# Local attention: VectorE copies the odd tiles' output out of PSUM at the head of a later iteration, ScalarE the even ones

## The chip, the cores and the metric

The kernel runs on one core of one Trainium2 chip. The time is the device's, in microseconds (us), from launch to end. The engines are named as the profile names them: PE (matrix multiply; PEld its weight loads), DVE (vector), ACT (scalar), POOL (GpSimd), SP (which here only issues DMAs). Each engine runs its own instructions in order and waits on semaphores.

## What is computed

Two recurrent blocks of a model over x of shape (4, 1024, 128), float32. Each block is `x = x + s * silu(f)`, where s is an attention branch and f a second branch, both of the layer-normed x. The change lies in the second branch of the second block: two layers (DEPTH = 2) of local attention with 8 heads of 64 channels and a window of 64, each followed by a gated feed-forward. Cut to what matters:

```python
h = shift_token(x)                      # second half of the channels comes from the token before
q, k, v = split(h @ wqkv)               # 8 heads x 64
q, k = rotary(l2norm(q) * qs, l2norm(k) * ks)
sim = einsum('bhwid,bhwjd->bhwij', bq, bk)      # 64 queries x 128 keys
attn = softmax(where(mask, -max, sim))
o = einsum('bhwij,bhwjd->bhwid', attn, bv)
x = x + o @ wo
h = layernorm(shift_token(x)) * lg + lb
...
x = x + (a * gelu(g)) @ w2 + b2
```

## The kernel before

The program is one loop over the 4 batches; within a batch the stages follow one another, and at its end the engines meet. All engines' instruction streams are written out by hand, in order, with semaphores between them: nothing reorders them.

The local attention of one layer works on T = 8 tiles of 128 tokens (a tile is two windows). Each engine runs a loop over u, and works in iteration u on several tiles at different depths. In what follows PS is the PSUM tensor with 8 banks of 512 words, and a number behind PS is the bank.

- PE, iteration u: the scores of tile u+1 into PS 0 to 3 (first the mask `band` as a matmul, then queries by keys); for tile m = u-3 the value matmuls "PV" into PS 6, which need both halves of the transposed probabilities (`pt`, `ptd`) and that tile m-1 has been copied out of PS 6 (`olT` at least m); for tile m = u-2 the transposes of the probabilities (L1480), four into PS 4 and four into PS 5; for tile q = u-4 the output product `wol` into PS 7, which needs `olT` at least q+1 and, since it overwrites the columns that the former tile used, that DVE has added the former tile (`xf`). Matmuls all carry the helper's line L1136; the trace names `x_in` as their input for `wol`, 64x128 forms for scores, 128x64 for PV.
- ACT, iteration u: 8 exps of tile u (L616), with the row sums; the copy of the first half of the transposed probabilities of tile u-2 (L624, `pt`); the copy of the attention output of tile q = u-3 from PS 6 into `olT` (L630). `olT` has two buffers, which lie where `x_in` was, so that the trace calls them `x_in`.
- DVE, iteration u: reciprocal of the sums and multiply of tile u-2 (L1069, L1071), which frees PE to transpose; max over the scores of tile u and a small product (L1077, L1079), which ACT needs for its exps; the add of tile u-6's output from PS 7 into `xf` (L1085), the own half of the shifted tensor (L1054) and the statistics of an earlier tile (L1062); the copy of the second half of the transposed probabilities of tile u-3 (L1095, `ptd`).
- SP: for each tile t from 0 to 6, once `xf` of the tile is there and the shift of the tile before has landed, two DMAs that write the shifted half of the channels into `tmp` (L372 and L374 or L376). DVE's statistics of the tile wait for them. Tile 7 is shifted by PE.

After the loop: layer norm, transposes, feed-forward, next layer.

Of the kernel before, what the change touches and what calls it, by code (L numbers as in the profile page):

```python
# [15 lines left out]
T = N // P  # L16
# [37 lines left out]
def build(nc, d, out):  # L54

    with ExitStack() as ctx:
# [3 lines left out]
        def sem(name):  # L60
            return ctx.enter_context(nc.semaphore(name))


        PS = ctx.enter_context(nc.psum_tensor("PS", [P, 8, HALF], F32))

        def pair(i):
            return PS[:, i:i + 2, :].rearrange("p a n -> p (a n)")
# [141 lines left out]
        olT = x_in[:].rearrange("p (q c) n -> p q c n", c=4)  # L209
# [19 lines left out]
        S = {n: sem(n) for n in names}  # L229
# [53 lines left out]
        def bc(v, shape, axis):  # L283
            return v.unsqueeze(axis).broadcast_to(shape)
# [170 lines left out]
        def _(act):  # L455
            act.wait_ge(S0["dve0"], 1)

            for i in range(2):
                for c in range(CH):
                    n = i * CH + c  # L460
# [13 lines left out]
            with act.Fori(0, B) as b:  # L474
# [40 lines left out]
                for k in range(2 * LOOPS):  # L515
                    for e in range(E):
# [5 lines left out]
                        for c in ((0, 1, 2, 3) if e == 0 else (2 * e + 2, 2 * e + 3) if e + 1 < E else ()):  # L522
                            n = k * FC + c
# [56 lines left out]
                for l in range(DEPTH):  # L580
                    for i in range(2):
                        act.wait_ge(S["hT_ps"], 16 * l + 4 * i + 4)
                        act.copy(hT[0:64, i * HALF:i * HALF + HALF], PS[0:64, 1 + i, :]).then_inc(S["hT"], 1)

                    if l == 0:
                        act.wait_ge(S["cleared"], 3)
                    for t in range(T + 4):
                        u = l * T + t
                        if t >= 4:
                            k, tt = u - 4, t - 4  # L590
                            act.wait_ge(S["kq_ps"], 2 * k + 1)
                            act.copy(qT[:, :, P * tt:P * tt + P], PS[:, 6, :].rearrange("p (c n) -> p c n", c=4))\
                                .then_inc(S["kq"], 1)
                            act.wait_ge(S["kq_ps"], 2 * k + 2)
                            act.copy(kT[:, :, WIN + P * tt:WIN + P * tt + P],
                                     PS[:, 7, :].rearrange("p (c n) -> p c n", c=4)).then_inc(S["kq"], 1)
                        if t < T:
                            act.wait_ge(S["rotb"], u + 1)
                            if u >= 2:
                                act.wait_ge(S["ssq"], u - 1)  # L600
                            act.activation(qk_sq[u % 2], pair(2 * (t % 2)), ACT.Square).then_inc(S["sq"], 1)  # L601
                            act.copy(vl[:, t], PS[:, 4 + t % 2, :]).then_inc(S["vl"], 1)  # L602
                        if 2 <= t <= T and t % 2 == 0:
                            k = t - 2
                            act.wait_ge(S["ssq_ok"], u // 2)
                            act.activation(rqt[:, k:k + 2], ssq[:, k:k + 2], ACT.Sqrt).then_inc(S["rq0"], 1)
                    for u in range(T + 4):
                        n = T * l + u
                        if u < T:
                            act.wait_ge(S["ml"], n + 1)  # L610
                            if n >= 3:
                                act.wait_ge(S["pt_ps"], 2 * (n - 2))
                            for r in range(2):
                                for c in range(4):
                                    h = 2 * c + r
                                    act.activation(pl[:, n % 3, r, c], PS[:, 2 * (n % 2) + r, KEYS * c:KEYS * c + KEYS],  # L616
                                                   ACT.Exp, bias=ml[:, n % 2, r, c:c + 1], scale=rq[:, u, h:h + 1],
                                                   accum_out=sl[:, n % 3, r, c:c + 1]).then_inc(S["p_exp"], 1)
                        if 2 <= u <= T + 1:
                            m = n - 2  # L620
                            if m >= 2:
                                act.wait_ge(S["o_lps"], m - 1)
                            act.wait_ge(S["pt_ps"], 2 * m + 1)
                            act.copy(pt[:, m % 2, 0], PS[:, 4, :].rearrange("p (c n) -> p c n", c=4)).then_inc(S["pt"], 1)  # L624
                        if 3 <= u <= T + 2:
                            q = n - 3
                            act.wait_ge(S["o_lps"], q + 1)
                            if q >= 2:
                                act.wait_ge(S["ol_ps"], q - 1)
                            act.copy(olT[:, q % 2], PS[:, 6, :].rearrange("p (c n) -> p c n", c=4))\  # L630
                                .then_inc(S["olT"], 1)

                    for i in range(2):
                        act.wait_ge(S["hT_ps"], 16 * l + 8 + 4 * i + 4)
                        act.activation(xT[:, i * HALF:i * HALF + HALF], PS[:, 1 + i, :], ACT.Identity,  # L635
                                       bias=res["ln_b"][:, l:l + 1], scale=res["ln_g"][:, l:l + 1])\
                            .then_inc(S["hT"], 1)
                    for i, (c, m) in enumerate(HC):
                        n = l * 3 + i
                        act.wait_ge(S["g_ps"], n + 1)  # L640
                        if n >= 2:
                            act.wait_ge(S["hg"], n - 1)
                        act.activation(gl[0:m, n % 2], PS[0:m, 3:5, :].rearrange("p a n -> p (a n)"), ACT.Gelu,
                                       bias=res["b1g"][0:m, l * 3 + i:l * 3 + i + 1]).then_inc(S["gl"], 1)
# [5 lines left out]
        def _(dve):  # L650
# [8 lines left out]
            def link(ins):  # L659
                k0[0] += 1  # L660
                ins.then_inc(S0["dve0"], 1)
                dve.wait_ge(S0["dve0"], k0[0])
# [8 lines left out]
            for i in range(2):  # L671
                for c in range(CH):
                    n = i * CH + c
# [91 lines left out]
            with dve.Fori(0, B) as b:  # L765
# [240 lines left out]
                for l in range(DEPTH):  # L1006
# [23 lines left out]
                    for t in range(T + 1):  # L1030
                        u = l * T + t
# [19 lines left out]
                    def own_half(t):  # L1051

                        dve.wait_ge(S["xf"], 2 * T * l + t + 1)
                        dve.tensor_copy(tmp[:, t, 0:64], xf[:, t, 0:64]).then_inc(S["hcp_v"], 1)  # L1054
# [8 lines left out]

                    for u in range(T + 6):
                        n = T * l + u
                        if 2 <= u <= T + 1:
                            m = n - 2
                            dve.wait_ge(S["p_exp"], 8 * (m + 1))
                            link(dve.reciprocal(rl[:, m % 3], sl[:, m % 3]))  # L1069
                            v = pl[:, m % 3]  # L1070
                            dve.tensor_tensor(v, v, bc(rl[:, m % 3], [P, 2, 4, KEYS], 3), ALU.mult).then_inc(S["pn"], 1)  # L1071
                        if u < T:
                            sv = PS[:, 2 * (n % 2):2 * (n % 2) + 2, :].rearrange("p r (c k) -> p r c k", k=KEYS)
                            dve.wait_ge(S["s_lps"], n + 1)
                            if n >= 2:
                                dve.wait_ge(S["p_exp"], 8 * (n - 1))
                            link(dve.tensor_reduce(ml[:, n % 2], sv, AX, ALU.max))  # L1077

                            dve.scalar_tensor_tensor(ml[:, n % 2], ml[:, n % 2], -1.0,  # L1079
                                                     rq[:, u, 0:HL].rearrange("p (c r) -> p r c", r=2),  # L1080
                                                     ALU.mult, ALU.mult).then_inc(S["ml"], 1)
                        if u >= 6:
                            t = u - 6
                            dve.wait_ge(S["ol_ps"], l * T + t + 1)
                            dve.tensor_tensor(xf[:, t], xs[:, t], PS[:, 7, 0:W], ALU.add).then_inc(S["xf"], 1)  # L1085
                            if t:
                                own_half(t - 1)
                            if t >= 2:
                                late_stats(t - 2)
                        if 3 <= u <= T + 2:  # L1090
                            m = n - 3
                            if m >= 2:
                                dve.wait_ge(S["o_lps"], m - 1)
                            dve.wait_ge(S["pt_ps"], 2 * m + 2)
                            dve.tensor_copy(pt[:, m % 2, 1], PS[:, 5, :].rearrange("p (c n) -> p c n", c=4))\  # L1095
                                .then_inc(S["ptd"], 1)
# [13 lines left out]
                    for i, (c, m) in enumerate(HC):  # L1110
                        n = l * 3 + i
# [536 lines left out]
```

## Time and profile before

| | us |
|---|---|
| median of 3 runs | 3063.28 |
| lowest and highest of them | 3052.27, 3063.64 |
| the profiled execution, its own time | 3055.92 |
| its span, first to last instruction | 3054.1 |

| engine | busy us | share of the span |
|---|---|---|
| PE | 2275.5 | 75% |
| DVE | 1975.2 | 65% |
| ACT | 1416.0 | 46% |
| POOL | 560.6 | 18% |

The shares are means over stages of different kinds; the local attention loops are 8 short stretches among them, the first from about 620 us to 674 us. The ACT copies in question are 64 of 585 to 842 ns each. Durations in the profile run from an instruction's start to the acknowledged end of its writes, and an engine starts its next instruction before that: what an instruction holds its engine for is the distance between starts.

### The profile page before, as it was taken

The numbers are of one execution on the slowest core, as the hardware profiler recorded it, in microseconds if no ns is written. First come the engines' busy times: TensorE is split into PE (matmuls) and PEld (weight loads), VectorE is DVE, ScalarE is ACT, GpSimd is POOL, SyncE is SP. The second block draws the span as 40 slices with busy tenths as digits, with TensorE's granted clock in tenths as the row PEclk, the third lists the DMA queues.
The fourth block names the chain that finished last, engine by engine and source line by source line (L and its number), as shares of the span: only waits on it lengthen the run. The fifth ranks groups of instructions, "written<-read, shape, count | busy, mean of one in ns | idle before, by whom it ended". The sixth has DMA issues, their size and how long they took to land.

```text
span 3054.1 us, 46022 instructions
## 1 busy us (share of the span) xinstructions
PE 2275.5 (75%) x17392; PEld 1277.1 (42%) x17392; DVE 1975.2 (65%) x4104; ACT 1416.0 (46%) x2537; POOL 560.6 (18%) x336
## 2 busy tenths in 40 slices
PE   4798588577779668767759948867767985885766
PEld 4576122254547412245546712225353751222545
DVE  5855696655674489565656568946566556966565
ACT  1333277264533347554623416746263332782544
POOL 0242000213043200041205300012212420003130
PEclk9999599778879879978779968978777985997878
DMA  3000200101000100010000020010100002001010
GB/s 132 1 1 1 74 16 9 28 6 26 11 9 1 53 22 19 8 27 11 21 17 1 1 69 19 7 22 16 22 17 8 1 1 74 16 9 30 5 26 18
DMA packets 52016, 65.13 MB, mean 21 GB/s; under 512 B 17696, under 2 KB 29216, under 8 KB 51264
## 3 DMA queue, kind: packets, MB, share of 16 engines
q1 hardware_dynamic: 48584, 56.18, 7.3%
q10 hardware_dynamic: 3192, 5.80, 0.6%
q8 instruction: 144, 2.36, 0.3%
q14 instruction: 96, 0.79, 0.1%
HBM read 25.19 MB, written 15.01 MB: 13 GB/s over the span
## 4 chain that ended last, share of the span: by engine, by line
PE 49%; DVE 23%; ACT 12%; DMA 6%; issue 5%; SPq 3%; POOL 2%; ACTq 0%; DVEq 0%; POOLq 0%
PE PS L1136 44%; DVE arena L971 9%; ACT arena L616 5%; DMA tmp<-xf 3%; ACT arena L571 2%; PE PS L1415 2%; PE PS L1154 1%; DVE s_at L1027 1%; DMA scr_k<-arena 1%; DVE tmp L996 1%; POOL arena L437 1%; DMA arena<-scr_k 1%; PE PS L1480 1%; SPq L344 1%; DVE arena L1044 1%
## 5 line engine op out<-in xcount | busy, mean ns | idle before, releaser
L1136 PE MATMUL PS<-arena 128*32 128x256 f32 (+4 forms) x10240 | 825.3, 356 | 204.4 <-DMA arena<-scr_k 75.3
L971 DVE TENSOR_REDUCE arena<-PS 128x1 f32<-128x512 f32 x1024 | 642.0, 684 | 101.7 <-PE PS L1136 101.7
L571 ACT ACTIVATE arena<-PS 128x1024 f32<-128x1024 f32 x512 | 515.6, 1033 | 306.7 <-PE PS L1136 306.7
L1136 PEld LDWEIGHTS PS<-arena 128*32 128x32 f32 (+4 forms) x10240 | 313.0, 124 | 714.9 <-DVE arena L971 282.9
L1136 PE MATMUL PS<-wqkv,arena 128*128 128x512 f32 x384 | 221.1, 730 | 65.4 <-ACT arena L602 56.2
L1136 PEld LDWEIGHTS PS<-w2e,arena 128*128 128x128 f32 x2048 | 246.0, 192 | 52.0 <-issue 51.7
L527 ACT ACTIVATE arena<-PS 128x512 f32<-128x512 f32 x256 | 150.7, 597 | 245.1 <-PE PS L1136 245.0
L1136 PE MATMUL PS<-w2e,arena 128*128 128x128 f32 x2048 | 246.8, 275 | 0.1
L616 ACT ACTIVATE arena<-PS,arena 128x128 f32<-128x128 f32 x512 | 230.0, 527 | 16.0 <-DVE arena L1079 16.0
L917 DVE TENSOR_TENSOR arena<-PS,arena 128x512 f32<-128x512 f32 x128 | 86.1, 689 | 213.2 <-PE PS L1136 212.8
L601 ACT ACTIVATE arena<-PS 128x1024 f32<-128x1024 f32 x64 | 65.5, 1023 | 325.1 <-DVE s_at L1027 248.5
L415 POOL TENSOR_TENSOR zz<-zz,arena 128x512 f32<-128x512 f32 x104 | 133.6, 1285 | 270.4 <-DVE arena L917 242.4
L421 POOL MEMSET arena<- 128x256 f32 x4 | 1.2, 311 | 924.9 <-ACT tmp L578 924.9
L1136 PEld LDWEIGHTS PS<-wqkv,arena 128*128 128x128 f32 x384 | 87.5, 241 | 167.2 <-issue 93.5
L616 ACT ACTIVATION_READ_ACCUMULATOR arena<-PS,arena 128x1 f32 x512 | 140.6, 275 | 0.0
L404 POOL TENSOR_TENSOR arena<-arena 128x1024 f32<-128x1024 f32 x32 | 75.1, 2346 | 282.2 <-ACT arena L503 274.2
L1136 PE MATMUL PS<-xT,w1e 128*128 128x512 f32 x256 | 120.5, 596 | 0.2
L1136 PE MATMUL PS<-x,w1e 128*128 128x512 f32 x256 | 120.5, 596 | 0.2
L1077 DVE TENSOR_REDUCE arena<-PS 128x8 f32<-128x1024 f32 x64 | 78.3, 1223 | 63.5 <-PE PS L1136 63.0
L1415 PE MATMUL PS<-ident,arena 128*128 128x128 f32 x256 | 54.0, 355 | 85.9 <-POOL arena L437 49.7
L1154 PE MATMUL PS<-ident,s_at 128*128 128x128 f32 x96 | 26.1, 452 | 121.2 <-DVE s_at L752 73.7
L450 POOL TENSOR_TENSOR tmp<-xf,b2f 128x1024 f32<-128x1024 f32 x8 | 18.7, 2341 | 488.2 <-ACT xT L635 488.2
(274 smaller groups left out, 3463.7 us busy)
## 6 DMA issues: line engine op xcount, KB each, us to landing
arena<-arena SPq DMA_DIRECT2D x120, 128.0 KB, 2.3
arena<-scr_k SPq DMA_DIRECT2D x28, 200.0 KB
arena<-scr_q SPq DMA_DIRECT2D x28, 192.0 KB
scr_q<-arena SPq DMA_DIRECT2D x16, 256.0 KB, 3.0
scr_k<-arena SPq DMA_DIRECT2D x16, 256.0 KB, 5.2
x_in<-in_x SPq DMA_DIRECT2D x5, 512.0 KB, 4.0
scr_q<-arena ACTq DMA_DIRECT2D x8, 256.0 KB, 4.9
scr_k<-arena ACTq DMA_DIRECT2D x8, 256.0 KB, 5.8
```

The lines of the kernel that those rows point to most:

```text
L404: pool.tensor_tensor(ub[:, c % 2], vsb[:, c % 2], bsb[:, c % 2], ALU.mult).then_inc(S["ub"], 1)
L415: pool.tensor_tensor(zz[:, half], src[:, half], ym[:, m % 4], ALU.add).then_inc(S["z"], 1)
L527: act.activation(hs[:, n % 8], PS[:, up_bank("up", k, c), :], ACT.Silu).then_inc(S["hs"], 1)
L571: act.activation(pb[:, n % 8], pair(2 * (n % 2)), ACT.Exp).then_inc(S["p"], 1)
L601: act.activation(qk_sq[u % 2], pair(2 * (t % 2)), ACT.Square).then_inc(S["sq"], 1)
L616: act.activation(pl[:, n % 3, r, c], PS[:, 2 * (n % 2) + r, KEYS * c:KEYS * c + KEYS], ACT.Exp, bias=ml[:, n % 2, r, c:c + 1], scale=rq[:, ...
L917: dve.tensor_tensor(ym[:, m % 4], PS[:, 4 + m % 4, :].rearrange("p (t w) -> p t w", w=W), bc(comb[:, half, e // EPG, e % EPG], [P, T // 2, ...
L971: dve.tensor_reduce(mxp[:, h % 2, j, t, hf:hf + 1], PS[:, ring_bank("mx", h, n), :], AX, ALU.max)\
L1077: link(dve.tensor_reduce(ml[:, n % 2], sv, AX, ALU.max))
L1136: return pe.matmul(o, w, v, start=start, stop=stop, **kw)
L1154: pe.transpose(PS[:, bank + t // 4, P * (t % 4):P * (t % 4) + P], src[:, t], ident[:])\
L1415: ins = pe.transpose(PS[:, 6 + i, P * c:P * c + P], qk_a[u % 4][:, HALF * i + P * c:HALF * i + P * c + P], ident[:])
```

## The change

Of the output copies PS 6 to `olT`, ACT keeps those of even tiles (q = u-3 in odd iterations). Those of odd tiles are taken by DVE, as the first instruction of the iteration after: in iteration u = 5, 7, 9 and 11 it copies tile q = u-4. Waits and the semaphore count (`olT`) are the same as those of ACT's copy. On both engines u's parity is that of the loop variable, and each layer's first tile is even.

```diff
-                        if 3 <= u <= T + 2:
+                        if 3 <= u <= T + 2 and u % 2 == 1:
                             q = n - 3
                             act.wait_ge(S["o_lps"], q + 1)
...
                     for u in range(T + 6):
                         n = T * l + u
+                        if 5 <= u <= T + 3 and u % 2 == 1:
+                            q = n - 4
+                            dve.wait_ge(S["o_lps"], q + 1)
+                            if q >= 2:
+                                dve.wait_ge(S["ol_ps"], q - 1)
+                            dve.tensor_copy(olT[:, q % 2], PS[:, 6, :].rearrange("p (c n) -> p c n", c=4))\
+                                .then_inc(S["olT"], 1)
                         if 2 <= u <= T + 1:
```

On ACT, from the exps of u=3 to those of u=6 of layer 0 (`x_in<-PS` is the olT copy, `arena<-PS 128x512` the pt copy), before:

```order
L616 ACTIVATE arena<-PS,arena 128x128 x8
L624 COPY arena<-PS 128x512
L630 COPY x_in<-PS 128x512
L616 ACTIVATE arena<-PS,arena 128x128 x8
L624 COPY arena<-PS 128x512
L630 COPY x_in<-PS 128x512
L616 ACTIVATE arena<-PS,arena 128x128 x8
```

and in the changed kernel, at the same place:

```order
L616 ACTIVATE arena<-PS,arena 128x128 x8
L624 COPY arena<-PS 128x512
L630 COPY x_in<-PS 128x512
L616 ACTIVATE arena<-PS,arena 128x128 x8
L624 COPY arena<-PS 128x512
L616 ACTIVATE arena<-PS,arena 128x128 x8
```

Every second olT copy is gone from ACT. On DVE, from the end of iteration 8 to the end of iteration 9 (`arena<-PS` the ptd copy, then reciprocal and multiply of tile 7, the add of tile 3), before:

```order
L1095 COPY arena<-PS 128x512
L1069 RECIPROCAL arena<-arena 128x8
L1071 TENSOR_TENSOR arena<-arena 128x1024
L1085 TENSOR_TENSOR xf<-xn,PS 128x128
L1054 COPY tmp<-xf 128x64
L1062 BN_STATS st<-tmp 128x6
```

and in the changed kernel, whose lines stand 7 lower from there on:

```order
L1102 COPY arena<-PS 128x512
L1071 COPY x_in<-PS 128x512
L1076 RECIPROCAL arena<-arena 128x8
L1078 TENSOR_TENSOR arena<-arena 128x1024
L1092 TENSOR_TENSOR xf<-xn,PS 128x128
L1054 COPY tmp<-xf 128x64
L1062 BN_STATS st<-tmp 128x6
```

The olT copy stands ahead of the reciprocal; at u=5 and u=7 it stands ahead of the max as well. PE's instructions are the same in both.

## Rows read from the trace of the kernel before

**Rows 1.** Busy time by window: us, PE, PEld, DVE, ACT, POOL busy (instructions), PEclk, DMA, GB/s.

```profile
639.24:656.51 17.27, 15.29 (x289) 13.62 (x280) 13.59 (x26) 17.27 (x73) 0.00 (x0) 1.00 0.03 7
```

**Rows 2.** Timeline of ACT: start, duration, engine, line, operation, idle before and its end.

```profile
643.19 0.65 ACT L630 COPY x_in<-PS 128x512 f32<-128x512 f32 x1
643.67 0.54 ACT L616 ACTIVATE arena<-PS,arena 128x128 f32<-128x128 f32 x1
...
647.16 0.70 ACT L624 COPY arena<-PS 128x512 f32<-128x512 f32 x1
...
648.10 0.60 ACT L616 ACTIVATE arena<-PS,arena 128x128 f32<-128x128 f32 x1
```

**Rows 3.** The chain that ended last, 620 to 680 us: start, duration, what.

```profile
657.78 0.29 DVE xf L1085
658.08 0.61 SPq L372
...
661.70 0.61 SPq L372
...
669.85 0.60 SPq L372
...
673.42 0.29 DVE st L1062
```

**Rows 4.** DVE's statistics, line 1062: idle before them until (us, times).

```profile
  DMA tmp<-xf: 39.6, 16
```

**Rows 5.** Timeline of DVE.

```profile
638.72 0.69 DVE L1095 COPY arena<-PS 128x512 f32<-128x512 f32 x1 [0.64 <-PE PS L1480]
...
639.33 0.19 DVE L1069 RECIPROCAL arena<-arena 128x8 f32<-128x8 f32 x1
...
641.95 0.17 DVE L1079 SCALAR_TENSOR_TENSOR arena<-arena 128x8 f32<-128x8 f32 x1
...
645.64 0.28 DVE L1085 TENSOR_TENSOR xf<-xn,PS 128x128 f32<-128x128 f32 x1
...
650.05 0.17 DVE L1079 SCALAR_TENSOR_TENSOR arena<-arena 128x8 f32<-128x8 f32 x1
650.14 0.28 DVE L1085 TENSOR_TENSOR xf<-xn,PS 128x128 f32<-128x128 f32 x1
...
656.40 0.20 DVE L1069 RECIPROCAL arena<-arena 128x8 f32<-128x8 f32 x1 [0.44 <-ACT arena L616]
```

**Rows 6.** Timeline of PE; x64 is scores and PV, `wol` the output product.

```profile
638.85 2.13 PE L1136 MATMUL PS<-arena 64*64 64x128 f32 x64
...
645.23 1.09 PE L1480 MATMUL PS<-ident,arena 128*128 128x128 f32 x8
646.16 1.06 PE L1136 MATMUL PS<-wol,x_in 128*128 128x128 f32 x8
647.43 0.41 PE L1136 MATMUL PS<-band,identb 64*64 64x512 bf16 x4 [0.21 <-ACT arena L616]
647.67 2.13 PE L1136 MATMUL PS<-arena 64*64 64x128 f32 x64
...
657.47 1.15 PE L1136 MATMUL PS<-arena 128*64 128x64 f32 x32 [1.43 <-ACT x_in L630]
```

**Rows 7.** Timeline of SP's DMA issues.

```profile
650.45 0.64 SPq L372 DMA_DIRECT2D tmp<-xf  x1
```

**Rows 8.** Busy time by window, columns as in rows 1: the granted clock (PEclk).

```profile
622.50:626.60 4.10, 0.02 (x4) 0.00 (x0) 1.70 (x4) 3.63 (x17) 0.00 (x0) 0.94 0.00 0
...
652.00:657.00 5.00, 3.07 (x48) 2.84 (x48) 3.10 (x8) 5.00 (x20) 0.00 (x0) 1.00 0.06 13
...
746.00:747.00 1.00, 0.08 (x1) 0.09 (x2) 1.00 (x2) 0.00 (x0) 0.86 (x1) 0.50 0.00 0
```

**Rows 9.** Timeline of PE between the two loops.

```profile
745.16 0.72 PE L1415 MATMUL PS<-ident,arena 128*128 128x128 f32 x4 [2.35 <-ACT arena L592]
```

## The prediction, made before the changed kernel ran

> **What bounds the kernel now.** The change touches one loop, the local attention, which runs 8 times (2 layers in each of 4 batches). I read first how busy each engine is in the middle of one such loop, then the chain that ended last over it, then who waits for its DMAs, and last the timelines of ACT, DVE and PE in it. All times below are of the first loop, in us from the span's start; "iteration u" is the loop variable of every engine, "tile m" the 128 tokens that a step works on.
>
> From 639.24 to 656.51 ACT is busy 17.27 of 17.27, PE 15.29, DVE 13.59 [rows 1]. So ACT is full in the middle of the loop: the exps of u=5 start at 643.67, those of u=6 at 648.10, a period of 4.43 [rows 2]. One olT copy holds ACT from 643.19 to 643.67, that is 0.48. By shares alone, moving it to DVE looks good.
>
> The chain of waits says more. It leaves ACT at the end of tile 7's exps, passes DVE (reciprocal and multiply of tile 7, then the add of tile 3 into xf at 657.78), and from there runs through the DMAs that shift xf by one row: issued at 658.08 for tile 3, at 669.85 for tile 6, landed at 673.42, where the last statistics can be taken [rows 3]. From tile 3's issue to that landing it is 15.34. Each DMA waits for the one before (3.62 from tile 3's issue to tile 4's at 661.70); DVE waits for them 39.6 us in all, twice in each of the 8 loops [rows 4]. So **the loop ends 15.34 after the add of tile 3**, as long as the later adds come no later than their DMAs. What matters is when DVE gets to that add.
>
> **The change part by part.** ACT loses 32 copies, DVE gains 32. The four odd tiles of a loop are copied by DVE as the first thing of u=5, 7, 9 and 11, and each copy waits for that tile's value matmuls (PV). Behind it on DVE are queued the multiply that lets PE transpose, the max that lets ACT start its exps, and the add into xf. No DMA moves, and nothing is moved past a queue of SP or POOL. The question is whether PV is done when DVE comes to the copy.
>
> Step 1, u=5. DVE is free at 639.33, which is where the reciprocal starts now [rows 5]. PV of tile 1 is the second half of the 64 matmuls that run from 638.85 for 2.13, to 640.98 [rows 6]. DVE waits 1.7 and starts the copy at 641.03. An existing copy of the same shape started at 638.72 and was followed, through reciprocal, multiply and max, by the small product at 641.95: 3.23 later. I give the new copy the same 3.23, since shape, source bank kind and engine agree: product at 644.26, done 0.17 later, its duration, and exps of u=5 at 644.46 (0.03 for the release) in place of 643.67. **Plus 0.8 us, where the bare saving on ACT would be minus 0.48.**
>
> Step 2, u=6 to u=7. After that product DVE does: the existing copy (0.09 later, as an add at 650.14 followed a product at 650.05), reciprocal (0.61 later, as 638.72 to 639.33), through to the next product (641.95 less 639.33 is 2.62), and the add of tile 0 at 647.67, done at 647.95; before it was at 645.64. PE's output product of tile 1 waits for that add, since it overwrites the same PSUM columns (before, it started at 646.16). It now starts at 648.0 and takes 1.06. The scores of tile 7 stand behind it on PE. They also need the exps of tile 5: before, they started at 647.43, 3.76 after 643.67, and waited for ACT [rows 2, 6]; so 648.2. PE's own queue is later: 649.1. Scores and PV together took from 647.43 to 649.80, 2.37 [rows 6]. PV of tile 3 ends at 651.5.
>
> Step 3, u=7. DVE copies tile 3 at 651.5, product at 654.73, exps of u=7 at 654.93. Before they came one period after 648.10, at 652.53: **plus 2.4**. The add of tile 1 is at 654.82, before 650.14: plus 4.7.
>
> Step 4, u=9. PV of tile 5 waited for an ACT copy and started at 657.47 [rows 6]. Now: exps at 654.93, ACT's copy pt 3.49 later (647.16 less 643.67), its olT copy of tile 4 0.48 after that, ending at 659.5. PE is ready at the same time: from the add of tile 1 (done 655.1) one output product, one PV, 8 transposes and another product, 1.06 + 1.15 + 1.09 + 1.06, give 659.5. PV of tile 5 runs 659.6 to 660.8. DVE's head copy starts at 660.85, the reciprocal 0.61 later, and the add of tile 3 comes 1.38 after the reciprocal (656.40 to 657.78): **662.84 in place of 657.78, plus 5.06**.
>
> Step 5, the DMAs. Tile 3's DMA goes out at 663.15, the last lands 15.34 later at 678.5 in place of 673.42. The later adds stay in front: by the same durations tile 5's comes near 669.4 (its DMA goes at 670.4) and tile 6's near 671 (DMA 674.9). The fourth head copy, at u=11, is hidden so; if that cover were gone it would cost its 0.6. After the loop comes a serial chain (layer norm, transposes, feed-forward), so nothing takes the delay back.
>
> Sum: 5.06 x 8 loops = **40.5 us on the profiled execution's 3055.9**, 3096.4. The profiled execution is one of the lower ones: with the three other runs the mean is 3058.7 and the median of the three is 3063.3. I add the 40.5 to the mean and round: **3100**.
>
> The bounds of the new wait are therefore not 0.69 (the copy's duration) on either side. From below: if PV were always done, the head copy would cost DVE 0.61 in a period of which it idles (17.27 - 13.59) / 4, about 0.9, so nothing, and ACT's saving stands. From above: every step as walked. I take the walk, because [rows 5, 6] put PV's end 1.65 after DVE is free already at the first odd tile.
>
> **A rule weighed.** The Trainium skill, TensorEngine Tiling (Array Packing), PSUM Bottleneck, says to use both ScalarE and VectorE to empty PSUM; Perfetto Trace Analysis, Identifying the Most-Contended Engine, says to optimize the engine of highest occupancy first. Both speak for this change: the trace agrees that ACT is the full one [rows 1]. They would give the first rival below. Neither looks at where in DVE's order the copy stands.
>
> **The rivals.**
>
> Rival 1, the head wait doesn't bind and the time is not slower. Then exps come 0.48 earlier after tile 1's copy is gone and 0.96 after tile 3's, and the add of tile 1 0.48 earlier. Its DMA, issued at 650.45 [rows 7], goes at 649.97, and two DMA steps of 3.62 put tile 3's at 657.2 in place of 658.08. That is 0.9 x 8, minus 7 us: 3052 on the mean. Even 32 x 0.48 is only 15.4. For it speaks ACT's full row [rows 1]. It decides on whether PV of an odd tile ends before DVE is done with the former iteration, and against that stands 640.98 against 639.33 [rows 5, 6]. Chance 7%.
>
> Rival 2, the wait is real but small: PE's order lets less of it through, for instance when only step 1's 0.8 and part of step 3 arrive, 1 to 2.4 per loop, 8 to 19 us: 3067 to 3078. Against it: steps 2 and 4 are queue order, not chance. Chance 8%.
>
> Rival 3, PE's clock falls. In step 3 PE idles from the end of its transposes (about 652.5) to the add at 655.1, 2.6 us. An idle of 4.1 early in the loop took the granted clock below 1.00, to a mean of 0.94 in that stretch, and the longest idle in the busy part, 1.43, left it at 1.00, which is 2.4 GHz [rows 6, 8]. But at 745.16 PE started after 2.35 of idle [rows 9], and from 746.00 the granted clock was 0.50, 1.2 GHz [rows 8]. So 2.6 lies where it can fall. Four steps of PE between there and tile 5's PV would cost 0.9 each more (bound: each at most doubles from 1.06 to 1.15), less 0.1 of slack, and that PV as much again: 3.4 to 4.4 a loop. In all loops, 27 to 35 us more: 3127 to 3135. Chance 17% for most loops; in a few loops it lies within my own range. The Trainium skill, TensorE: Matmul & The Clock Gate, says that idle gaps bring the engine back to its slow state and warns of micro-idles between groups; the rows agree that it can happen, and no run here yet shows it in this place.
>
> **How the numbers follow.** Forecast 66%, with its own range of 3085 to 3118: the base is 3052 to 3064, and the walk is good to some 1.5 us a loop (15.34 is 0.9 more than four DMA steps of 3.62, so that much may not come again). Rivals 1 to 3 have 7, 8 and 17%, other causes 2%. The range 3076 to 3132 leaves out rival 1, most of rival 2 and the far end of rival 3, about 2 in 10. Slower by over 0.5% (15 us, about what a measurement of this kernel can tell from no change): 66 + 17, half of rival 2 and 1 of the rest, 88%. Within 0.5%: the other half of rival 2 and 6 of rival 1, 10%. Faster: 2%.
>
> **What would show it.** In the changed kernel: DVE's new copy waits for PE, near 1.7 at u=5, 3.0 at u=7 (DVE is free at about 648.5) and 1.8 at u=9; the exps of u=5 and u=7 wait for DVE, where they waited for nothing, and those of u=7 start about 10.5 after those of u=5 (8.9 before); the add of tile 3 comes 5 later, and the DMA stretch behind it is unchanged near 15.3. PE's clock stays at 1.00 until the loop's end. The forecast is wrong if the new copy finds PV done, if ACT's exps follow without idle, or if the DMA stretch shrinks so that it eats the delay.

## The result, and the profile after

| | before | after |
|---|---|---|
| median, us (4 runs each) | 3058.71 | 3109.70 |
| lowest to highest | 3052.27 to 3063.64 | 3105.60 to 3114.52 |
| span of the profiled execution | 3054.1 | 3107.5 |

The ratio is 1.0169, with a 95% interval of 1.014 to 1.0197. The change costs 51 us by the medians, 53.4 by the spans. The forecast was plus 40.5, 3100.

The trace of after runs 0.72 us ahead of the one of before when the first loop starts (its first max at 620.79, before at 621.51), so 0.72 is to be added to its times before they are compared with those of before. First DVE's timeline; `COPY x_in<-PS` on L1071 is the new copy, L1086 the small product, L1092 the add into xf.

```profile
640.31 0.69 DVE L1071 COPY x_in<-PS 128x512 f32<-128x512 f32 x1 [1.61 <-PE PS L1143]
...
643.54 0.17 DVE L1086 SCALAR_TENSOR_TENSOR arena<-arena 128x8 f32<-128x8 f32 x1
...
646.93 0.28 DVE L1092 TENSOR_TENSOR xf<-xn,PS 128x128 f32<-128x128 f32 x1
...
650.83 0.69 DVE L1071 COPY x_in<-PS 128x512 f32<-128x512 f32 x1 [3.02 <-PE PS L1143]
...
654.14 0.28 DVE L1092 TENSOR_TENSOR xf<-xn,PS 128x128 f32<-128x128 f32 x1
...
661.39 0.69 DVE L1071 COPY x_in<-PS 128x512 f32<-128x512 f32 x1 [1.47 <-PE PS L1143]
...
663.37 0.28 DVE L1092 TENSOR_TENSOR xf<-xn,PS 128x128 f32<-128x128 f32 x1
```

The head copies wait 1.61, 3.02 and 1.47 us for PE. Over the program all 32 do:

```profile
L1071 DVE COPY x_in<-PS x32: 690/692/693, 640.3 to 3061.9; 128x512 f32<-128x512 f32 x32
...
  PE PS L1143: 58.6, 32
```

ACT, which had no gap before its exps in this part of the loop [rows 2], now waits for DVE's product before u=5 and u=7:

```profile
643.74 0.46 ACT L616 ACTIVATE arena<-PS,arena 128x128 f32<-128x128 f32 x1 [1.09 <-DVE arena L1086]
...
654.25 0.46 ACT L616 ACTIVATE arena<-PS,arena 128x128 f32<-128x128 f32 x1 [1.91 <-DVE arena L1086]
```

With the 0.72 added these are 644.46 and 654.97. PE's timeline, in which the output product of tile 2 starts at 654.56:

```profile
648.65 2.13 PE L1143 MATMUL PS<-arena 64*64 64x128 f32 x64
650.71 1.09 PE L1487 MATMUL PS<-ident,arena 128*128 128x128 f32 x8
654.56 1.13 PE L1143 MATMUL PS<-wol,x_in 128*128 128x128 f32 x8 [2.76 <-DVE xf L1092]
655.62 1.60 PE L1143 MATMUL PS<-arena 128*64 128x64 f32 x32
657.16 1.97 PE L1487 MATMUL PS<-ident,arena 128*128 128x128 f32 x8
658.92 1.35 PE L1143 MATMUL PS<-wol,x_in 128*128 128x128 f32 x8
660.20 1.15 PE L1143 MATMUL PS<-arena 128*64 128x64 f32 x32
```

After the idle of 2.76 us PV takes 1.60 where it took 1.15 [rows 6], the transposes 1.97 against 1.09, the output product 1.35 against 1.06. The windows (us, PE, PEld, DVE, ACT, POOL busy, then the granted clock) say why: the granted clock was below the 1.00 of [rows 8], and from 656.20 to 659.50 it was 0.50, the 1.2 GHz level.

```profile
652.00:657.00 5.00, 2.44 (x40) 2.35 (x40) 4.92 (x11) 3.09 (x14) 0.00 (x0) 0.91 0.03 6
657.00:662.00 5.00, 5.00 (x60) 4.70 (x58) 1.30 (x2) 1.96 (x7) 0.00 (x0) 0.75 0.06 12
656.20:659.50 3.30, 3.30 (x31) 3.18 (x28) 1.06 (x5) 2.76 (x10) 0.00 (x0) 0.50 0.04 8
```

The chain that ended last goes, as in [rows 3], from the add of tile 3 into the DMAs:

```profile
663.37 0.29 DVE xf L1092
663.68 0.61 SPq L372
...
667.31 0.61 SPq L372
...
670.91 0.60 SPq L372
...
674.91 0.61 SPq L372
...
678.47 0.29 DVE st L1062
```

From tile 3's issue to the last landing it is 14.79 in this first loop, before 15.34. DVE waits for these DMAs 39.8 us in all, before 39.6 [rows 4].

All eight loops show this. The table gives, for every kernel of this study, the start of an add, or of the first statistics' aggregate (L744), which ends the loop, counted from the loop's first max, as the mean over the 8 loops of its trace:

| kernel | add of tile 1 | of tile 3 | of tile 7 | aggregate | ratio to before |
|---|---|---|---|---|---|
| before | 28.61 | 36.24 | 45.97 | 52.47 | |
| after | 33.32 | 42.55 | 52.09 | 58.63 | 1.0169 |
| late_copy | 28.62 | 35.30 | 45.02 | 51.72 | 0.9991 |
| wait_only | 32.12 | 39.54 | 48.50 | 55.62 | 1.0095 |
| first_two_on_dve | 33.32 | 40.44 | 49.41 | 56.14 | 1.0105 |
| last_two_on_dve | 28.64 | 39.15 | 48.69 | 55.24 | 1.0067 |
| warm_pe | 33.25 | 41.27 | 50.82 | 57.22 | 1.0109 |
| two_dma_chains | 28.62 | 36.26 | 45.98 | 49.06 | 0.9906 |
| two_chains_late_copy | 28.62 | 35.28 | 45.01 | 48.13 | 0.9888 |
| two_chains_head_copy | 33.31 | 42.55 | 52.10 | 55.39 | 1.0088 |
| two_chains_late_warm | 28.62 | 35.31 | 45.03 | 48.10 | 0.9856 |

So the loops account for (58.63 - 52.47) x 8 = 49.3 of the 53.4 us between the spans; 4.1 lie outside the loops. The feed-forward's first 16 matmuls (`PS<-xT,wf`), which run partly at the low clock, take 9.08 us after a loop of the changed kernel and 8.72 before, means of 8. That would be 2.9 of the 4.1, if all of it reaches the end, which isn't shown.

What a loop's end gains or loses is not passed on one to one. From the first max of a batch's first loop to that of its second the traces have, as means over the 4 batches: before 136.59, after 143.46, late_copy 136.57, wait_only 140.05, first_two_on_dve 140.09, last_two_on_dve 140.03, warm_pe 139.48, two_dma_chains 133.19, two_chains_late_copy 133.16, two_chains_head_copy 140.03, two_chains_late_warm 129.60. A loop that ends 2.77, 3.15 or 3.67 late thus makes the next one 3.44, 3.46 or 3.50 late, and one that ends 0.75 early makes it 0.02 early. Sums of a loop's delay times 8 are approximate for that reason.

### The profile page after: what moved, and what is told of

Same layout as the page of the kernel before. It is cut to its first block, busy times and chain, and to the rows that moved or that the text cites. A ratio compares the mean times of both kernels' runs of the same rounds, so it can differ in the third digit from the quotient of the medians.

```text
span 3107.5 us, 46022 instructions
## 1 busy us (share of the span) xinstructions
PE 2292.4 (74%) x17392; PEld 1290.0 (42%) x17392; DVE 1989.3 (64%) x4136; ACT 1403.3 (45%) x2505; POOL 561.1 (18%) x336
## 4 chain that ended last, share of the span: by engine, by line
PE 51%; DVE 24%; ACT 8%; issue 6%; DMA 6%; SPq 3%; POOL 2%; ACTq 0%; DVEq 0%; POOLq 0%
PE PS L1143 46%; DVE arena L971 9%; DMA tmp<-xf 3%; ACT arena L616 2%; ACT arena L571 2%; PE PS L1422 2%; PE PS L1487 2%; PE PS L1161 1%; DVE arena L1084 1%; DVE s_at L1027 1%; DMA scr_k<-arena 1%; DVE tmp L996 1%; POOL arena L437 1%; DMA arena<-scr_k 1%; DVE arena L1044 1%
## 5 line engine op out<-in xcount | busy, mean ns | idle before, releaser
L616 ACT ACTIVATION_READ_ACCUMULATOR arena<-PS,arena 128x1 f32 x512 | 115.4, 225 | 0.0
```

## The experiments

My theory (A): the place at the head of DVE's iteration costs, since the copy waits there for PE with everything that ACT and PE need queued behind it. Rivals: the work of four more copies on DVE; every head copy the same; only what delays ACT; and for the part of the delay beyond the forecast, PE's clock.

### late_copy

The changed kernel, with the copy moved within DVE's iteration:

```diff
                     for u in range(T + 6):
                         n = T * l + u
-                        if 5 <= u <= T + 3 and u % 2 == 1:
...
                         if 2 <= u <= T + 1:
...
+                        if 5 <= u <= T + 3 and u % 2 == 1:
...
                         if 3 <= u <= T + 2:
                             m = n - 3
```

> Edit: the changed kernel, but DVE's copy of an odd tile's output stands at the end of the iteration, ahead of the ptd copy, instead of at its head. Theory A (the place in DVE's order costs, not the engine): PV of tile 1 ends at 640.98, the copy would come at 642.0, so it waits for nothing; ACT keeps its relief of 0.48 per odd tile, the adds of tiles 1 and 3 come 0.4 to 1.0 earlier than in the kernel before, and a loop ends 0.4 to 0.8 us earlier: 3 to 6 us below before, ratio to before 0.998 to 0.999. Theory B (DVE is too full for four more copies of 0.61): 2.4 us of DVE a loop, slower than before by up to 20 us, ratio up to 1.006.

Measured: 3052.03 us against 3053.93, ratio 0.9991, interval 0.9976 to 1.0006. The work is the same as in the changed kernel, on the same engines; the cost is gone. The 32 copies on DVE wait for PE 6.9 us in all, where they waited 58.6:

```profile
  PE PS L1143: 6.9, 16
```

DVE's timeline of this kernel at u=5, where the copy (here L1095) follows the product with no wait:

```profile
638.58 0.17 DVE L1079 SCALAR_TENSOR_TENSOR arena<-arena 128x8 f32<-128x8 f32 x1
638.67 0.68 DVE L1095 COPY x_in<-PS 128x512 f32<-128x512 f32 x1
639.27 0.68 DVE L1102 COPY arena<-PS 128x512 f32<-128x512 f32 x1
```

ACT's exps of u=5 and u=7 in it follow its pt copy at once, 8.40 apart where they were 8.86 apart before:

```profile
639.84 0.52 ACT L616 ACTIVATE arena<-PS,arena 128x128 f32<-128x128 f32 x1
...
648.24 0.62 ACT L616 ACTIVATE arena<-PS,arena 128x128 f32<-128x128 f32 x1
```

The trace shows a gain of 0.94 at the add of tile 3 and 0.75 at the loop's end. It goes no further: the next layer's loop starts 136.57 after this one, before 136.59, and the feed-forward's first 16 matmuls take 9.1 where they took 8.7. Of the 3.9 us between the spans (3050.2 and 3054.1), 3.3 lie ahead of the first loop, which the edit doesn't touch (its first max at 618.20, before at 621.51). The timed runs can't tell the ratio from 1 either. They do exclude the 1.006 of theory B. The 0.4 expected at the add of tile 1 did not come: with two copies in a row on DVE the add of tile 0 comes 0.24 later than before, counted from the first max (642.57 less 618.20, against 645.64 less 621.51), and the output product and the scores stand behind it on PE. That this takes the 0.4 back is my reading; no run tests it alone.

### wait_only

The kernel before, with one wait more:

```diff
                     for u in range(T + 6):
                         n = T * l + u
+                        if 5 <= u <= T + 3 and u % 2 == 1:
+                            dve.wait_ge(S["o_lps"], n - 3)
```

> Edit: the kernel before with all copies on ACT, and DVE only waits at the head of u=5, 7, 9 and 11 for PV of tile u-4. It shows the wait without the copy's work and without ACT's relief. Theory A: the wait is the larger part. Walk from the rows of before: exps of u=5 at 643.85, of u=7 at 653.67 (1.1 late), the add of tile 3 at 660.9, 3.1 late; 25 us over 8 loops, 10 more if PE's clock falls in the idle of 2.0 us before tile 2's output product. Ratio 1.008 to 1.011. Theory B (the work of the copies costs, the wait is filled anyway): no change from before, 1.000.

Measured: 3084.18 us, ratio 1.0095, interval 1.0075 to 1.0115. The instruction behind the wait is now the reciprocal (here L1071), and PE idles 2.17 before tile 2's output product (L1138):

```profile
639.08 0.20 DVE L1071 RECIPROCAL arena<-arena 128x8 f32<-128x8 f32 x1 [1.61 <-PE PS L1138]
...
649.00 0.20 DVE L1071 RECIPROCAL arena<-arena 128x8 f32<-128x8 f32 x1 [3.02 <-PE PS L1138]
...
652.14 1.13 PE L1138 MATMUL PS<-wol,x_in 128*128 128x128 f32 x8 [2.17 <-DVE xf L1087]
...
657.75 0.20 DVE L1071 RECIPROCAL arena<-arena 128x8 f32<-128x8 f32 x1 [1.58 <-PE PS L1138]
```

The add of tile 3 comes at 39.54, that is 3.30 late (3.1 expected). The clock stayed at 1.00 from 652 to 662, so the 10 us that were reserved for its fall did not come. A wait that adds no work at all costs a loop 3.15 us at its end. That is half of the changed kernel's 6.16, and it refutes theory B. An estimate of the rest: three copies of 0.61 that now lie on the path (1.83), and the clock (1.28, below): 3.15 + 1.83 + 1.28 = 6.26. This sum leaves out ACT's relief, so it shows sizes and is no proof of each.

### first_two_on_dve and last_two_on_dve

The changed kernel with only half of the copies moved, `if u in (5, 7):` or `if u in (9, 11):` on DVE and the other odd tiles left with ACT.

> Edit: only tiles 1 and 3 are copied by DVE at the head (u=5, 7); ACT keeps tiles 5 and 7. Theory A: exps of u=7 come 2.4 late and the add of tile 1 4.7 late as in the changed kernel; the shift DMAs start from the latter and hold the loop's end 4.4 late: 35 us, ratio 1.010 to 1.013. PE's clock falls as in the changed kernel, hidden behind the DMAs. Theory B (each head copy costs the same): half of the changed kernel's 51 us, ratio 1.008.

> Edit: only tiles 5 and 7 are copied by DVE at the head (u=9, 11); ACT keeps tiles 1 and 3. Theory A: exps are untouched; the head copy at u=9 waits for PV of tile 5 (657.47 + 1.15), so the add of tile 3 comes at 660.65, 2.9 late, its DMA 2.6 to 2.9 late: 21 to 23 us, ratio 1.007; PE's clock stays at 1.00 through the loop. Theory B (each head copy costs the same): half of 51 us, ratio 1.008; theory C (only what delays ACT costs): 1.000.

Measured: the first two 3088.61 us, ratio 1.0105 (1.0086 to 1.0125); the last two 3077.70 us, ratio 1.0067 (1.0043 to 1.0092). The intervals overlap, and the second holds theory B's 1.008, so it is the traces that tell them apart.

With the first two, the add of tile 1 is at 33.32, exactly as in the changed kernel, and the clock falls as there:

```profile
657.00:662.00 5.00, 5.00 (x54) 4.76 (x53) 2.71 (x8) 3.99 (x16) 0.00 (x0) 0.66 0.04 9
```

The loop ends 3.67 late; 4.4 was expected. Part of the 4.71 at the add of tile 1 is made up behind it, where the add of tile 3 is 4.20 late. With the last two, exps and the add of tile 1 are untouched (28.64), and the head copy at u=9 alone pushes the add of tile 3:

```profile
659.03 0.69 DVE L1071 COPY x_in<-PS 128x512 f32<-128x512 f32 x1 [2.71 <-PE PS L1143]
659.64 0.19 DVE L1076 RECIPROCAL arena<-arena 128x8 f32<-128x8 f32 x1
...
661.01 0.28 DVE L1092 TENSOR_TENSOR xf<-xn,PS 128x128 f32<-128x128 f32 x1
```

It comes 2.91 late (2.9 expected), the loop's end 2.77. That ACT must be delayed for it to cost (theory C) is refuted: ACT is not. Nor does each head copy cost the same (theory B): all that arrives at the end is there at the add of tile 3, before the head copy of u=11, which waits for PE too but stays hidden behind the DMAs. The two halves give 3.67 + 2.77 = 6.44, the whole 6.16.

### warm_pe

The changed kernel, with work for PE in its idle time; the results of the added transposes are not used.

```diff
                                 ins.then_inc(S["pt_ps"], 1)
+                        if u == 6:
+                            pe.wait_ge(S["p_exp"], 8 * (n + 1))
+                            for k in range(16):
+                                pe.transpose(PS[:, 0, P * (k % 4):P * (k % 4) + P], ident[:], ident[:])
```

> Edit: the changed kernel with 16 additional transposes of the identity into a free PSUM bank, in PE's idle time after the transposes of tile 4 in u=6; their result isn't used. Theory A (PE's clock falls because of the 2.8 us of idle there, and that costs the 1.25 us a loop by which the add of tile 3 came later than forecast): the granted clock stays at 1.00 through 652 to 662, the add of tile 3 comes 41.3 after the loop's first max instead of 42.6, and the time is about 10 us below the changed kernel's, 3099, ratio to before 1.013. Theory B (the clock falls for another reason, or the 1.25 has another cause): no change from the changed kernel, ratio 1.017.

Measured: 3086.66 us, ratio 1.0109, interval 1.0092 to 1.0126. PE does 128 matmuls more, and the program is faster than the changed kernel. The timeline of PE (L1492 are the added ones), and then the windows:

```profile
650.79 1.97 PE L1492 MATMUL PS<-ident 128*128 128x128 f32 x16
653.44 1.13 PE L1143 MATMUL PS<-wol,x_in 128*128 128x128 f32 x8 [0.68 <-DVE xf L1092]
654.50 1.15 PE L1143 MATMUL PS<-arena 128*64 128x64 f32 x32
655.58 1.09 PE L1487 MATMUL PS<-ident,arena 128*128 128x128 f32 x8
```

```profile
652.00:657.00 5.00, 4.32 (x60) 3.93 (x59) 4.02 (x11) 3.87 (x17) 0.00 (x0) 1.00 0.03 7
657.00:662.00 5.00, 3.28 (x51) 2.85 (x50) 3.38 (x8) 1.31 (x3) 0.00 (x0) 1.00 0.05 10
```

The clock stays at 1.00, and the add of tile 3 comes at 41.27: 1.28 earlier than in the changed kernel, and 5.03 later than before, where the forecast had 5.06. So the part of the loop's delay beyond the forecast is PE's clock. The gain of the whole program is larger than the 10 us expected, 18 by the ratios. The two traced executions are 25.5 apart (this one is the fastest of its five): 11.3 in the loops (1.41 x 8), the rest outside them, with the program's mean granted clock at 0.860 where the changed kernel has 0.849. Why the clock was higher outside the loops this study didn't test.

### two_dma_chains

The kernel before, with the shift DMAs on two semaphores by the parity of their number:

```diff
-                        if n:
-                            sp.wait_ge(S["hsh"], 32 * n)
+                        hs_ = S["hsh2" if n % 2 else "hsh"]
+                        if n >= 2:
+                            sp.wait_ge(hs_, 32 * (n // 2))
```

with DVE's wait before the statistics changed alike.

> Edit: the kernel before, with two semaphores for the shift DMAs, so that tile t's waits for tile t-2's instead of tile t-1's. Theory A (the loop's end is set by the chain of serial DMAs, 3.62 us each, from the add of tile 3): each DMA goes when its add is done, the last at 666.2 instead of 669.85, and a loop ends 3.6 us earlier: 29 us, ratio 0.990. Theory B (the landing of a DMA and not its issue is serial, or something else ends last): 0 to 5 us.

Measured: 3026.65 us, ratio 0.9906, interval 0.9893 to 0.992. The adds come when they came before (45.98 for tile 7), and the loop ends 3.41 earlier. DVE's wait for the DMAs, 39.6 us before [rows 4], is down to:

```profile
  DMA tmp<-xf: 12.8, 8
```

This confirms the reading of the chain in the prediction: what ended a loop was the serial DMAs, from the add of tile 3 on.

### two_chains_late_copy and two_chains_head_copy

Both changes together: the two DMA chains with DVE's copies late, and with DVE's copies at the head as in the changed kernel.

> Edit: two DMA chains and the odd tiles' copies on DVE at the end of the iteration. Theory A: with the DMAs no longer serial, the loop's end follows the last adds, which ACT's relief of 0.96 by u=7 brings forward: 0.9 us a loop below two DMA chains alone, ratio to before 0.988. Theory B (the relief is lost in the tail, where ACT waits for PE): the same as two DMA chains alone, 0.990.

> Edit: the changed kernel with two DMA chains. Theory A: the add of tile 7 comes 6.1 us later a loop in the changed kernel than in the one before; with two chains the loop's end follows it, so this kernel lies 6.1 x 8 = 49 us above two DMA chains alone: ratio to before 1.006. Theory B (the delay of the head copies only counts through the DMA chain): level with two DMA chains alone, 0.990.

Measured: late 3022.20 us, ratio 0.9888 (0.9873 to 0.9903); head 3084.35 us, ratio 1.0088 (1.007 to 1.0106). With the DMAs no longer serial, the late copy's gain at the loop's end is 49.06 - 48.13 = 0.93 a loop, where it was 0.75. Again it does not reach the next loop (133.16 against 133.19), and by the intervals it can't be told from two DMA chains alone. The head copy costs 55.39 - 49.06 = 6.33 a loop here, so its delay doesn't count through the DMA chain alone: all adds are late, and whatever follows the last one is late too. In time it is 57.7 us above two DMA chains alone, more than the 49 expected; 51 of it in the loops. That refutes theory B.

### two_chains_late_warm

The surprise of warm_pe, put to use: two_chains_late_copy with 38 unused transposes after the loop's last matmul on xf, where PE idles for the layer norm.

```diff
                     mm(PS[:, 7, W:W + 64], shift_in[:], xf[:, T - 2, 64:W], start=False).then_inc(S["sh_ps"], 1)
+                    for k in range(38):
+                        pe.transpose(PS[:, 0, P * (k % 4):P * (k % 4) + P], ident[:], ident[:])
```

> Edit: two DMA chains and the late copy, and 38 additional transposes of the identity into a free PSUM bank, in the 5.8 us in which PE idles after the loop for the layer norm; their result isn't used. Theory A (the idle lowers PE's clock and the feed-forward's first matmuls pay for it): the granted clock stays at 1.00, the first 16 matmuls with 512 columns take 7.2 us in place of 9.26, 2 us less a layer, 16 us over the 8 loops: ratio to before 0.983 to 0.984. Theory B (the clock falls all the same, or the stage waits for ACT and DVE): as two chains with the late copy, 0.989.

Measured: 3007.22 us, ratio 0.9856, interval 0.9834 to 0.9877, the fastest kernel of the study. The loops are unchanged (48.10); the stage behind them is shorter. PE's timeline after the loop in this kernel:

```profile
664.65 4.32 PE L1505 MATMUL PS<-ident 128*128 128x128 f32 x38
670.58 2.12 PE L1163 MATMUL PS<-ident,s_at 128*128 128x128 f32 x8 [1.61 <-DVE s_at L753]
673.57 7.14 PE L1145 MATMUL PS<-xT,wf 128*128 128x512 f32 x16 [0.87 <-ACT xT L636]
```

and without the added transposes:

```profile
670.08 2.27 PE L1163 MATMUL PS<-ident,s_at 128*128 128x128 f32 x8 [5.76 <-DVE s_at L753]
673.21 9.26 PE L1145 MATMUL PS<-xT,wf 128*128 128x512 f32 x16 [0.87 <-ACT xT L636]
```

The feed-forward's first 16 matmuls take 7.14 in place of 9.26, as expected, in the first layer of each of the 4 batches. In the second layers it is 8.24 in place of 9.18, since the last four wait for DVE:

```profile
809.57 1.98 PE L1145 MATMUL PS<-xT,wf 128*128 128x512 f32 x4 [0.83 <-DVE arena L1123]
```

So these matmuls give about 12 us, not 16. In all, the traced execution, the fastest of its four, has 3.6 us less from the first loop to the second (129.60 against 133.16); where the other 1.5 come from isn't shown. The ratio came out at 0.9856 where 0.983 to 0.984 was expected; its interval holds the upper end of that. It excludes 0.989, theory B's value, but overlaps narrowly with the interval of two_chains_late_copy (0.9873 to 0.9903), which was timed on another occasion: that there is a gain rests on the trace as much as on the times.

## Why the prediction was right, and where it was short

**What bounds.** Right. The loop ends with the serial DMAs after the add of tile 3; two_dma_chains shows it by taking them apart. They are not needed for the cost, though: two_chains_head_copy loses as much without them.

**Step 1.** Right to a hundredth: exps of u=5 at 644.46 on the clock of before, as forecast, after a wait of 1.61 at the head copy (1.7 forecast).

**Steps 2 and 3.** Right: the head copy of tile 3 starts at 650.83 + 0.72 = 651.55 (651.5 forecast), exps of u=7 at 654.97 (654.93), the add of tile 1 at 654.86 (654.82). The coupling through PSUM, by which the output product waits for the add that DVE does last, was part of this walk: without it the scores of tile 7 would have waited for the exps alone, 648.2 in the forecast's count in place of 649.1. No run takes this coupling out by itself.

**Step 4.** Its structure was right, one duration was not: it gave PE's four steps after its idle their durations at the full clock, 4.36 in all. They took from 654.56 to 660.20, 5.64. The add of tile 3 came 6.31 late in place of 5.06. This is the term that was mis-sized, by 1.25 x 8 = 10 us, and warm_pe, which keeps the clock up, brings it back to 5.03. The forecast's sign that PE's clock would stay at 1.00 until the loop's end failed.

**Rival 3.** It was priced as another case than the forecast, with 17%; what happened is the forecast's path with rival 3's clock, in all 8 loops. The price given for it, 3.4 to 4.4 a loop, was three times too high: the clock was low from about 656 to 659, and touched three steps by 0.45, 0.88 and 0.29, not five steps by 0.9 each. The clue in [rows 8, 9], that 2.35 us of idle had been enough elsewhere, deserved more than 17%.

**Step 5 and the sum.** The DMA stretch of the first loop shrank by 0.55, within the 0.9 that was allowed for it; with the means over the loops 6.16 of the 6.31 arrive at the end. The rest of the difference, 4.1 us outside the loops, no step of the forecast had. The measured 3109.7 lies in the forecast's own range of 3085 to 3118.

**Rivals 1 and 2.** Neither happened. Rival 1 is what late_copy does: it decided on whether PV was done when DVE came to the copy, and moving the copy to where PV is mostly done takes the cost away. Rival 1's gain of 7 us isn't seen: the ratio gives 3, with an interval from -7 to +2, and the trace shows that the loops' gain doesn't reach the next loop. That late_copy's 3052.03 is the 3052 of rival 1 is luck, since that time was counted from a higher base.

**The rule that spoke for the change** (the Trainium skill, TensorEngine Tiling (Array Packing), PSUM Bottleneck: use both engines to empty PSUM) holds in late_copy inside the loop only, with 0.75 us that don't reach the next one, and fails by 51 us at the head of the iteration. By the other (the Trainium skill, Perfetto Trace Analysis, Identifying the Most-Contended Engine) ACT was to be relieved first; the chain of waits, not ACT's full row, named what ended the loop, and taking it apart was worth 30 us.

## What to carry to other kernels

A wait costs what is queued behind it on its engine. Before moving an instruction to a less busy engine, look in the timeline whether its input is ready when that engine gets there; within one iteration, put it behind the work that others wait for. Then follow the coupling through every buffer: here the add that frees PSUM columns stood behind the waiting copies too, and waits of 1.6, 3.0 and 1.5 us made a loop 6 us longer. And where an engine is full in the middle of a stage, check by the chain of waits whether the stage ends with it at all, and by the start of the next stage whether a gain gets that far.

## What the runs showed of the hardware that was not expected

- PE's granted clock fell after an idle of 2.76 us in the loop, in all 8 loops of the changed kernel; it stayed at 1.00 after 2.17 in wait_only, in all 8 loops too, after 1.43 before the change, and after 0.68 in warm_pe. The length of one idle doesn't settle it alone: in the kernel before, the clock fell 2.0 us after the loop's last matmul had ended (668.50), as the two windows below show.

```profile
668.50:670.40 1.90, 0.00 (x1) 0.00 (x0) 0.39 (x2) 0.00 (x0) 0.00 (x0) 1.00 0.00 0
670.50:674.00 3.50, 0.00 (x0) 0.00 (x0) 0.55 (x3) 0.00 (x0) 0.00 (x0) 0.50 0.05 9
```

- 128 unused matmuls in the 2.76 us of idle made the changed kernel 18 us faster by the ratios (1.0169 to 1.0109).
- Filling 4.3 of PE's 5.8 us idle after the loop took 2.1 us from the feed-forward's first 16 matmuls in the first layers, which had run partly at the low clock (9.26 to 7.14), and 0.9 in the second layers. The Trainium skill, TensorE: Matmul & The Clock Gate, The HAM clock gate, tells that an idle engine goes back to the low clock; warm_pe and two_chains_late_warm agree.
